# Moving the attention's P·V bursts from odd to even key tiles in a fused attention and FFN kernel

## The reference

```python
def attn(x, Wqkv, bqkv, Wproj, bproj):
    q, k, v = split(x @ Wqkv + bqkv)          # 16 heads of 64
    a = softmax(where(causal, q @ k.T * 64**-0.5, -inf))
    return (a @ v).merge_heads() @ Wproj + bproj
def ffn(x, W, b, V_r, C):
    return x @ W.T + b + (x @ V_r) @ C.T      # V_r, C of rank 32
x = x + attn(layernorm(x), ...)
x = x + ffn(layernorm(x), ...)
```

## Time and profile before

| | us |
|---|---|
| median of 3 runs | 850.07 |
| lowest, highest | 845.58, 889.94 |
| the profiled execution | 847.23 |
| its span on the slowest core (core 2) | 845.7 |
| spans of the eight cores | 839.1 to 845.7 |

### The profile page before, as it was taken

One profiled execution on the slowest core, in us unless ns is written; L12 is line 12 of the kernel. 1 busy time (PEld: TensorE's weight loads), 2 busy tenths in 40 slices (PEclk: granted clock), 3 DMA queues, 4 the chain that ended last, 5 costly groups with the idle time before them and its releaser, 6 DMA issues.

```text
span 845.7 us, 10497 instructions; the slowest of 8 cores (839.1 to 845.7 us)
## 1 busy us (share of the span) xinstructions
PE 656.0 (78%) x3433; PEld 280.8 (33%) x3433; DVE 288.6 (34%) x717; ACT 333.0 (39%) x449; POOL 185.5 (22%) x304
## 2 busy tenths in 40 slices
PE   0399999999137778788787977878888888966666
PEld 0144444444023323333232332333333333322322
DVE  2543534301023443435234323232313232243342
ACT  0031323222004465546355565656676757500000
POOL 2000000000104524515322222222222222213211
PEclk9999999999655578889988989989898898968798
DMA  8991210000762000000100001010101010102001
GB/s 161 208 212 52 72 29 26 0 1 1 113 111 75 1 1 1 26 26 26 50 26 26 29 22 51 0 50 1 51 1 51 1 50 2 51 26 74 26 25 50
DMA packets 15125, 38.13 MB, mean 45 GB/s; under 512 B 3401, under 2 KB 3425, under 8 KB 15073
## 3 DMA queue, kind: packets, MB, share of 16 engines
q0 software_dynamic: 7616, 11.67, 9.0%
q1 hardware_dynamic: 7457, 25.79, 8.9%
HBM read 39.68 MB, written 8.39 MB: 57 GB/s over the span
## 4 chain that ended last, share of the span: by engine, by line
PE 63%; DVE 15%; issue 7%; ACT 6%; POOL 5%; DMA 4%; DVEq 1%; SPq 0%; ACTq 0%; POOLq 0%
PE ps_pv L403 14%; PE ps_sc L251 13%; PE ps_sc L420 7%; PE ps_pv L276 7%; PE ps_w L549 4%; PE ps_w L626 4%; PE ps_bf L235 4%; PE ps_pv L626 4%; DVE wq_a L488 3%; DMA xf_a<-wffn 3%; POOL xf_a L440 3%; ACT xf_a L429 2%; ACT xnt_a L429 2%; PE ps_sc L549 2%; DVE xnt_a L458 2%
## 5 line engine op out<-in xcount | busy, mean ns | idle before, releaser
L429 ACT ACTIVATE xf_a<-ps_sc 128x1024 bf16<-128x1024 f32 (+1 forms) x192 | 167.0, 893 | 125.0 <-PE ps_sc L420 123.5
L420 PE MATMUL ps_sc<-q_fm,k_fm 64*128 64x512 bf16 (+3 forms) x640 | 123.4, 404 | 53.2 <-ACT xf_a L429 28.3
L429 ACT ACTIVATE xnt_a<-ps_sc 128x1024 bf16<-128x1024 f32 (+3 forms) x128 | 112.3, 897 | 121.6 <-PE ps_sc L420 121.0
L403 PE MATMUL ps_pv<-xf_a,v_on 128*66 128x512 bf16 (+3 forms) x384 | 114.0, 395 | 9.6 <-POOL xf_a L440 5.6
L251 PE MATMUL ps_sc<-xnt_a,wq_a 128*128 128x512 bf16 x512 | 115.5, 385 | 0.9 <-DVE xnt_a L317 0.9
L440 POOL TENSOR_TENSOR xf_a<-xf_a,tri_sb 128x128 bf16<-128x128 bf16 x152 | 60.6, 427 | 193.2 <-ACT xf_a L429 193.0
L403 PE MATMUL ps_pv<-xnt_a,v_on 128*66 128x512 bf16 (+3 forms) x256 | 77.1, 396 | 5.1 <-POOL xnt_a L440 2.5
L420 PEld LDWEIGHTS ps_sc<-q_fm,k_fm 64*128 64x128 bf16 x640 | 31.1, 96 | 149.2 <-issue 145.6
L440 POOL TENSOR_TENSOR xnt_a<-xnt_a,tri_sb 128x128 bf16<-128x128 bf16 x104 | 42.1, 431 | 175.4 <-ACT xnt_a L429 175.2
L251 PEld LDWEIGHTS ps_sc<-xnt_a,wq_a 128*128 128x128 bf16 x512 | 50.1, 99 | 60.3 <-issue 4.4
L210 ACT ACTIVATE ln_t<-mv,eps_t 128x1 f32<-128x1 f32 x32 | 9.3, 290 | 144.0 <-DVE mv L205 144.0
(11 more groups left out here) (65 smaller groups left out, 592.9 us busy)
## 6 DMA issues: line engine op xcount, KB each, us to landing
xf_a<-x SPq DMA_DIRECT2D x32, 512.0 KB, 3.7
y<-xf_a SPq DMA_DIRECT2D x16, 512.0 KB, 2.7
wq_a<-wqkv POOLq DMA_DIRECT2D x3, 2048.0 KB, 40.1
wq_a<-wproj POOLq DMA_DIRECT2D x1, 2048.0 KB, 19.4
xf_a<-wffn POOLq DMA_DIRECT2D x4, 512.0 KB, 25.5
bias_a<-bqkv POOLq DMA_DIRECT2D x1, 512.0 KB, 57.1
bias_a<-bffn POOLq DMA_DIRECT2D x1, 512.0 KB, 62.5
bias_a<-bproj SPq DMA_DIRECT2D x1, 512.0 KB, 5.7
```

What stands on the lines that cost most here:

```text
L403: e.matmul(ps_pv[hd][0:66, off * 128:512], v_on[:, ki2, 66 * hh:66 * hh + 66], chunkpair(cp)[:, hd * 512:hd * 512 + ncol], start=st, stop=sp),
L420: e.matmul(ps_sc[:, pp * 1024 + hd * 512 + off * 128: pp * 1024 + hd * 512 + 512], k_fm[hp:hp + 64, hc, ki * 128:(ki + 1) * 128], q_fm[hp: ...
L429: e.activation(chunkpair(cp).rearrange("p (a n) -> p a n", a=2) [:, :, 0:ncol], ps_sc[:, pp * 1024:(pp + 1) * 1024] .rearrange("p (a n) -> ...
```

## The change

The bursts of P·V matmuls are issued on even key tiles instead of odd ones. The threshold of six entries and the drain are the same.

```diff
--- before.py
+++ after.py
@@ -444,7 +444,7 @@
                                     waits=[m_ex, m_cm], sig="pl")
                     pend.append((cp, off, ncol, gate, ki, hd))
                 gki += 1
-                if ki % 2 == 1:
+                if ki % 2 == 0:
                     pop_pv()
                 pump()
             pop_pv(drain=True)
```

## The result

The changed kernel takes 873.21 us (median of 10 runs, 871.83 to 881.13), the kernel before, with its own ten, 847.21: a ratio of 1.032, 95% interval 1.0291 to 1.0348. That is 26.0 us slower where 19.9 were forecast; direction and range held, and 867 was 6 us short. Runs in which the cores of one die ran at a lower clock are left out of all ratios here (of e6 two of four runs were such; its two others gave 850.36 and 848.60).

The account below looks back on a forecast made before the run. TensorE was taken as busiest, 656.0 of 845.7 us, with little-filled pairs paced by ScalarE's exponentials. Terms 16.4 + 1.6 - 1.3 + 1.2 + 2.0 = 19.9 us on 847.23 gave 867; 8-in-10 range 854 to 880.

Parts of the forecast that it names:

- Group 0 at zero: First query group (K=4): no filler, order on TensorE identical, so zero change.
- The uncovered steps: Filler steps waiting for VectorE's read of ps_w lose the burst ahead: 25 at 0.655 us, 9 at 0.18; 16.4 + 1.6 us.
- The two gains: K=12, pair 0: two waiting filler steps, at tiles 4 and 6, gain a burst ahead of them; -1.3 us.
- The pair ends: K=16 pairs with full filler: mask products start later against tile 12; +0.3 us a pair, 4 pairs, 1.2 us.
- the 2.2 to 2.6 that were to show it: Sign of the forecast: the full pairs should each be 2.2 to 2.6 us longer.
- Little-filled pairs: Pairs with little filler, paced by ScalarE's exponentials: zero for K=12 and 16, 2.0 us for K=8.
- K=8, +2.0: Little-filled K=8 pairs 0, 1, 2, 4 and 7: later tile 7 exponentials, +0.4 us each, 2.0 us.
- the case's own 861 to 873: Range of the forecast case around 867 us, given chance 0.58.
- Rival (a): Part of the loss is absorbed, as at pair ends waiting for GpSimd: half of 19.9, 857 us; chance 0.22.
- (d): Nothing happens, VectorE's reads are not what holds the filler steps: 849 us; chance 0.05.
- (b): Short stalls bring the clock down once more in each of 7 full pairs: 12.6 us more, 879 us; chance 0.11.
- (c): Moved bursts fill waits at pair starts and keep the clock up: 28.8 us saved against 19.9 lost, 838; chance 0.04.

Follow-up runs that it names:

- e6: Kernel before with two P·V matmuls on every key tile instead of four on every other, filler as before; 850.36 and 848.60 us, no interval.
- e1: Changed kernel (bursts on even tiles) with one more empty step in each c job of the filler; 837.67 us, ratio 0.9896.
- e2: Kernel before (bursts on odd tiles) with one more empty step in each c job of the filler; 865.86 us, ratio 1.0229.
- e12: e11 with bursts on even key tiles and e5's empty step in the c jobs; 801.60 us, ratio 0.9455.
- e3: Kernel before with bursts on even tiles only in the odd-numbered (full) pairs of groups 2 and 3; 871.37 us, ratio 1.0295.
- e4: Kernel before with bursts on even tiles in all pairs except the odd-numbered ones of groups 2 and 3; 847.36 us, ratio 1.0001.
- e5: e1 with VectorE's copy of the transposes directly behind them in a1 and c, the empty step behind it; 834.0 us, ratio 0.9833.
- e7: Kernel before with the next pair's first two tiles' scores and exponentials issued ahead of this pair's drain; 859.55 us, ratio 1.0129.
- e11: e7 with the normalization behind key tile 2 instead of behind the drain, and e5's order of transposes and copies; 802.35 us, ratio 0.9439.

## Why the prediction was right, and where it was short

**Group 0 at zero.** Right: 47.2 and 47.1 us.

**The uncovered steps.** Right in mechanism and number, a little low in size: 16.4 + 1.6 - 1.3 = 16.7 us forecast, 17.9 more in the waits of the two slowest cores, 17.8 as the mean over all cores; 32 waits more forecast, 31 counted. That these waits are the loss, and not the bursts' place, is shown by e1, e2 and e12; that they sit in the full pairs, by e3 and e4. The two gains came too: group 2, pair 0 is 2.0 us shorter, 1.3 of it on ps_w. Two things made the term too small. The forecast took 0.655 us for every 512-wide read. In the full pairs the filler starts 1.01 to 1.09 us behind the start of the scores, however wide these are, so behind the narrower scores of a diagonal tile the gap is up to 0.85: K=12, pairs 3, 5 and 7 show 0.21, 0.69, 0.68 and 0.85, 2.43 us, where K=16 shows 2.21. And it took the bracket for the loss, where the start distances give 0.07 to 0.08 more for each gap; for 31 gaps that is 2 us (an estimate from the rows at 643.97 to 650.36).

**The pair ends.** K=16, +0.3 a pair: in group 3, pairs 5 and 7, the part from the scores of tile 12 to the next pair grew from 5.79 and 5.61 us to 6.44 and 6.26 (medians over the cores), 0.65 where 0.75 was forecast, and 0.45 left the part ahead: +0.2. These two pairs are 2.65 and 2.68 us longer in all, a little more than the 2.2 to 2.6 that were to show it. K=12: the full pairs 3, 5 and 7 of group 2 are 2.7 to 3.0 longer. No wait for GpSimd is visible in them before or after; what the forecast lacked there is the wider gap of the diagonal tile.

**Little-filled pairs.** K=12 and 16 at zero: the seven medians are -0.1 to +0.8, 1.7 us together, which is within what e4 can tell. K=8, +2.0: this term was wrong. Group 1 grew by 1.0 in all, and with its own three uncovered steps in there, 1.6 us, its other parts gave back 0.6. Pairs 0, 1 and 4 grew by 0.2 to 0.8 where 0.4 was forecast, but pair 2 fell by 1.6 and pair 7 by 0.4; on five of the eight cores pair 2 has no time at the lower clock, where all had 3.4 us before.

**What was missing: the clock, other waits and the tail.** TensorE's idle time in the attention rose by 20.4 us (82.1 to 102.5, mean over the cores). 17.8 are the waits above and 2.8 longer waits for ScalarE on L420 (52.1 to 54.9), which the forecast had left out; the others together are a little shorter. The time at half clock rose by 5.6 (134.3 to 139.9); TensorE is busy in 118.1 us of it against 115.1, which costs 1.5. The attention grew by 23.1 (481.1 to 504.2), and the 1.2 that are left are of the kind of the start distances above. Most of the clock's share is one pair, group 2, pair 1, here of the kernel before and of that after:

```profile
421.90:441.40 19.50, 18.08 (x103) 7.53 (x102) 6.06 (x17) 10.79 (x12) 5.94 (x10) 0.81 0.06 25
```

```profile
421.50:444.50 23.00, 19.00 (x103) 7.94 (x102) 6.06 (x17) 10.62 (x12) 6.54 (x10) 0.78 0.06 24
```

It grew by 3.5 here and 4.1 in the median, of which 1.7 are gaps of the forecast's kind, 0.8 is a wait for ScalarE, and the rest goes with 4.1 us more at the lower clock. In group 3, pair 3, the clock went the other way: no time at the lower level after against 3.4 before, and the pair grew by only 1.4. The tail's 1.3 us (5 on two cores) is the clock too. On the six cores the lower level lasts as long as before (37.7 us against 37.6) and TensorE's idle time is the same, but its stretches fall on other work: TensorE is busy in 28.2 to 29.6 us of them, before in 25.5 to 26.9. On the two others it lasts 48.2 us; one of them is the slowest core, with 0.79 in the last row of the stages. Why it is granted otherwise there was not tested. The forecast had put the clock in a rival only; where the sum fell short is that it took the clock and the waits for ScalarE as unchanged and every gap as 0.655 us. The 2.0 us for K=8, which did not come, hid part of this, so that 867 is as near as it is partly by luck; 873.21 lies just above the case's own 861 to 873 and inside the 854 to 880.

**Rival (a)**, half absorbed, is out: the waits' 17.9 us all arrive, and with them **(d)** is out. **(b)**, the clock falling by the short gaps, is out as well. The stretch of the full pair above:

```profile
644.00:662.00 18.00, 15.79 (x75) 5.68 (x74) 3.21 (x6) 8.93 (x10) 0.81 (x2) 1.00 0.07 30
```

TensorE idles for 2.2 of 18 us in four gaps, and the clock is 1.00 throughout. In the seven full pairs, before and after, on every core, the lower level sets in 1.4 to 3.8 us into the pair or not at all; it never sets in at or behind the new gaps. The Trainium skill, "TensorE: Matmul & The Clock Gate", "A second HAM failure mode: psum-queue depth-cycling", tells of a kernel in which micro-idles between matmul groups made the clock swing; gaps of 0.2 to 0.7 us 4.2 to 4.5 us apart did not do it here. **(c)**, faster by the clock at the pairs' starts, did not come with this change, but its mechanism is real: e12 has 65 us at the lower level instead of 134, and of the 46 us that it is faster some 28 are less busy time of TensorE.

## What to carry to other kernels

A block of independent work in an in-order queue is cover for whatever the queue waits for next: count which waiting instructions stand behind it before moving it, and move them with it (e1, e5, e12) or leave both. Where a wait is removed, look on every engine for what was hidden beneath it: e7 took most of ScalarE's wait away, met 2 us of VectorE's work, and became slower until that was moved as well. A chain of small waits at each stage boundary costs more than its length if the clock drops behind it.

## What the runs showed of the hardware that I had not expected

In these traces the granted clock goes with a pair's start and not with the gaps of up to 0.85 us inside a full pair. Two waits for ScalarE of about 1 us in a row (group 3, pair 2; the earlier trace rows show the second) were followed by 3 to 6 us at 0.50, while four gaps of up to 0.69 us in 18 us left it at 1.00. It is no fixed rule: group 3, pair 3 begins with a wait of 1.05 us in both kernels and has 3.4 us at the lower level before and none after. In e11 and e12, with the starts' waits gone, the full pairs 3, 5 and 7 of group 3 have no time at the lower level on any core. 67.8 and 64.7 us of it remain of 134.3 (mean over the cores), over a quarter of them in group 0. The attention of e12 is 45.9 us shorter than before. 17.5 of them are idle time. The other 28.4 are busy time: TensorE is busy in 54.2 us at the lower level instead of 115.1, and half of that difference is 30.
